# One subtraction per step on GpSimd, low products a step later, first key tiles loaded earlier, in a two-layer graph attention kernel

## The chip, the cores and the metric

The kernel runs on one core of a Trainium2 chip. The metric is the device time of one execution in microseconds (us), as the median of several runs. An engine is named by its role: TensorE (PE in the profile), VectorE (DVE), ScalarE (ACT), GpSimd (POOL), SyncE (SP, which issues DMA transfers).

## The reference

```python
# x: 4096 x 512, adj: 4096 x 4096; both layers: h = relu(layernorm(x)), 8 heads of 64
# layer 0: leaky additive scores + adj, softmax, times the projected rows; added to x
...
# layer 1, added to x again
keys = jnp.einsum('nj,hjk->hnk', node_matrix, Wks)
queries = jnp.einsum('nj,hjk->hnk', node_matrix, Wqs)
values = jnp.einsum('nj,hjk->hnk', node_matrix, Wvs)
atts = jnp.einsum('hqk,hmk->hqm', queries, keys) / key_dim ** 0.5
atts = atts - 1e+16 * (1.0 - adj)[None, :, :]
atts = jax.nn.softmax(atts, axis=-1)
return jnp.einsum('hqm,hmk,hko->qo', atts, values, Wo)
```

The diff concerns layer 1 alone.

## The kernel before, in words

`build` runs four stages one after another: projection and attention of layer 0, then `layer1_project` and `layer1_attention`. Each stage is a block in which every engine has its own hand-written instruction order; engines meet only through semaphores that count, and a stage ends when all its engines are done.

**Numbers.** Scores and sums need more precision than one fp16 product gives, so operands are split in a high and a low fp16 part. Keys are kept twice: KA holds, for each parity of head pair and each head x, the high part on partitions 0 to 63 and the low part on 64 to 127; KB holds the high part on partitions 0 to 63, and constant rows that carry the negated row maximum. The exponential of a score tile is written twice by ScalarE: in fp32 to PF (L1550) and in fp16 to PH (L1554). PL = PF - PH is the low part, subtracted by GpSimd, one tile of 128 x 512 an instruction (`split`, L1501 to L1505).

**`layer1_project`** walks 8 blocks of 512 rows. SyncE stores each query and key tile (high and low) to DRAM scratch (L989), loads the finished 512 columns of the first head pair's keys to KA's parity 0 (`load_first_keys`, L969 to L977), stores the V tiles (L995) and in block 0 loads queries. TensorE and VectorE use those first keys for the first head pair's guards (below, L1197 and L1072) within this stage.

**`layer1_attention`** walks NB = 8 blocks of 512 query rows, in each HP = 4 head pairs, in each NT = 32 key tiles of 128 rows: a *step* is one key tile for both heads of a pair, 1024 steps in all, two tiles (t) a step. The order of a step on TensorE (`body`, L1807 to L1843):

- `scores` for x = 0 and 1: two 512-column matmuls each (L1740, L1741) into one of three PSUM banks, and a third (L1743) that adds the mask, unless VectorE adds it (L1683; in pair 0 every second tile, later 3 of 8). A bank is free when the exponential of three tiles before is done.
- *guards*: score matmuls of the **next** head pair without softmax (L1724), 64 a head pair in steps 1 to 28, of which VectorE takes masked row maxima (L1594). After the last one VectorE reduces them (L1602) and negates and scales them (L1604, `merge_guards`); in step 30 TensorE turns them into a row (`crow`, L1729 to L1733), which VectorE writes into QL (L1610) for the next pair's scores.
- `products` of the step LAG = 2 before: 16 high matmuls of 65 or 64 columns with PH (L1761, L1763), then 8 low ones of 65 columns with PL (L1771), which wait for GpSimd. At their end the step counts as used, which frees slots of PH and PL (8 tiles) and pieces of V.
- `finish` for the pair before: its accumulators are copied in step 2 (ScalarE L1530, VectorE L1615), normalised in step 3 (L1621 reciprocal, L1623 multiply), transposed in step 5 (L1780), split in step 7 (L1629, L1631), and after the fourth pair multiplied by Wo (L1789, 48 matmuls).

ScalarE takes tiles in order: wait for the scores or VectorE's mask, wait for PF's slot (4 tiles, freed by GpSimd), L1550, L1554. VectorE's order is written by hand too: finish, guard maxima, masks. In the last two head pairs of a block it also sets up masks of the next one (`mask_setup` L1572, L1575; `mask_diagonal` L1583). SyncE's queue reloads KA, KB, V, masks and queries group by group (a group is 8 key tiles) as they come free; at the start of the stage it issues, for each of 4 groups, KB of the first pair, the mask MT, V, and KA of the second pair (L1428 to L1434). Guards from step 1 on read KA of the second pair.

Of the kernel before, what the change touches and what calls it, by code (L numbers as in the profile page):

```python
# [885 lines left out]
def layer1_project(nc, T, DR):  # L886
# [4 lines left out]
    with ExitStack() as ctx:  # L891
# [10 lines left out]
        s_KA, s_Q, s_MR, s_dblk, s_mk, s_fill = (T[name] for name in ("s_KA", "s_Q", "s_MR", "s_dblk", "s_mk", "s_fill"))  # L902
# [48 lines left out]
        def _(sp):  # L951
# [26 lines left out]

            load_first_rows()
# [3 lines left out]
            for g in range(NB):  # L983
                for j in range(PAIRS):

                    sp.wait_ge(s_lo, g * PAIRS + (j + 1))
                    row, i, to = (j % HP) * P, j % RING, "qk"[j // HP]
                    for half, tile in (("h", hi), ("l", lo)):
                        sp.dma_start(DR[to + half][row:row + P, bass.ds(g * QB, QB)], tile[:, i, :]).then_inc(s_qout[i], 16)  # L989
                if g == 0:  # L990
                    load_first_queries(0)
                load_first_keys(g)
                for s in range(SUB):
                    sp.wait_ge(s_v, g * SUB + (s + 3))
                    sp.dma_start(DR["v1"][:, bass.ds(g * QB + s * P, P), :].rearrange("h p k -> p h k"),  # L995
                                 vt[:, s, :, :].rearrange("p (h a) k -> p h (a k)", a=2)).then_inc(s_vout, 16)
                if g == 0:
                    load_first_queries(1)
            for i in range(RING):
                sp.wait_ge(s_qout[i], 32 * (NB * PAIRS // RING + 1))  # L1000
# [254 lines left out]
def layer1_attention(nc, T, DR):  # L1255
# [11 lines left out]
    F_RING, H_RING = 4, 8  # L1267
# [36 lines left out]
    POOL_SLOTS = (0, 1, 2, 3)  # L1304
    PER_RING = (F_RING - len(POOL_SLOTS), len(POOL_SLOTS))
    SPLITS = tuple(n * TILES // F_RING for n in PER_RING)

# [7 lines left out]
    def keys_landed(par, count):  # L1315

        return 64 * (count + (2 if par == 0 else 1))

    def by_pool(t):
        return t % F_RING in POOL_SLOTS  # L1320

    def split_count(t):

        return sum(by_pool(k) == by_pool(t) for k in range(t + 1))

    with ExitStack() as ctx:
# [10 lines left out]
        s_KA, s_Q, s_MR, s_dblk, s_mk, s_fill = (T[name] for name in ("s_KA", "s_Q", "s_MR", "s_dblk", "s_mk", "s_fill"))  # L1337
# [25 lines left out]
        s_KB = [sem(f"kb_in{i}") for i in range(GROUPS)]  # L1363
# [5 lines left out]
        s_low = sem("low_by_vector")  # L1369
# [57 lines left out]
        def _(sp):  # L1427
            sp.dma_start(idh[:, :], DR["idh"]).then_inc(s_fill, 16)  # L1428
            for i in range(GROUPS):
                load_kb(sp, 0, i)  # L1430
                load_mt(sp, 0, i)
                load_v(sp, 0, i)
                load_ka(sp, 1, 1, i)
# [55 lines left out]
            for par in range(2):  # L1489
                for i in range(GROUPS):  # L1490
                    sp.wait_ge(s_KA[par][i], keys_landed(par, 2 * NB))
            for hp in range(HP):
                sp.wait_ge(s_Q[hp], 96 * (NB + (1 if hp < 2 else 0)))
            for i in range(GROUPS):
                sp.wait_ge(s_KB[i], 32 * (HP * NB + 1))
                sp.wait_ge(s_V[i], 16 * (HP * NB + (1 if i < GROUPS - 1 else 0)))
                sp.wait_ge(s_MT[i], 16 * (NB + (1 if i < GROUPS - 1 else 0)))
# [3 lines left out]
        def split(eng, engine, nb, t):  # L1501

            engine.wait_ge(s_P, nb * TILES + (CREDIT + t + 1))
            eng.tensor_tensor(PL[:, t % H_RING, :], PF[:, t % F_RING, :], PH[:, t % H_RING, :],  # L1504
                              ALU.subtract).then_inc(s_lowp if by_pool(t) else s_low, 1)  # L1505

        @block.gpsimd
        def _(pool):
            pool.memset(shift[D:D + 2, :], P_SHIFT / C_ROW).then_inc(s_fill, 1)
            pool.sem_inc(s_lowp, PER_RING[1])  # L1510
            for nb in range(NB):
                for t in range(TILES):
                    if by_pool(t):
                        split(nc.gpsimd, pool, nb, t)

        @block.scalar
        def _(act):
# [14 lines left out]
            def body(nb, first):  # L1532
                for hp in range(HP):
                    for mb in range(NT):
# [7 lines left out]
                        for x in range(2):  # L1542
                            t = hp * PAIR + 2 * mb + x
                            if masked_by_vector(t):
                                act.wait_ge(s_M, nb * vector_masks(TILES - 1) + vector_masks(t))
                            else:
                                act.wait_ge(s_S, nb * TILES + (CREDIT + t + 1))

                            act.wait_ge(s_lowp if by_pool(t) else s_low, nb * SPLITS[by_pool(t)] + split_count(t))
                            nc.scalar.activation(PF[:, t % F_RING, :], sc[(nb * TILES + t) % BANKS][:, :], ACT.Exp, scale=EXP_SCALE)  # L1550

                            if x == 0:
                                act.wait_ge(s_used, nb * STEPS + (hp * NT + mb + 1))
                            nc.scalar.activation(PH[:, t % H_RING, :], sc[(nb * TILES + t) % BANKS][:, :], ACT.Exp, scale=EXP_SCALE).then_inc(s_P, 1)  # L1554
# [6 lines left out]
        def _(dve):  # L1561
            nc.vector.tensor_copy(only[D:D + 2, :], T["identf"][D:D + 2, D:D + 2]).then_inc(s_set, 1)
            nc.vector.tensor_scalar(idm[:, :], T["identf"][:, :], -MASK_FLOOR, None, ALU.mult).then_inc(s_set, 1)
            if PER_RING[0]:
                dve.sem_inc(s_low, PER_RING[0])
# [97 lines left out]
            def body(nb, first):  # L1663
                for hp in range(HP):
                    for mb in range(NT):
# [6 lines left out]
                        for x in range(2):  # L1672
                            t = 2 * (step - 1) + x
                            if t >= 0 and not by_pool(t):
                                split(nc.vector, dve, nb, t)
                            elif t < 0 and not first and not by_pool(t + TILES):
                                split(nc.vector, dve, nb - 1, t + TILES)
# [24 lines left out]
            for x in range(2):  # L1702
                if not by_pool(TILES - 2 + x):
                    split(nc.vector, dve, NB - 1, TILES - 2 + x)
# [4 lines left out]
        def _(pe):  # L1709
# [4 lines left out]
            def guard(it, nxt, gi, count, blk):  # L1714
# [4 lines left out]
                if s == 0 and x == 0 and c % (MC // GROUPS) == 0:  # L1719
                    pe.wait_ge(s_KA[par][c // (MC // GROUPS)], keys_landed(par, count))  # L1720
# [25 lines left out]
            def products(nb, step):  # L1746
# [9 lines left out]
                first, last = mb == 0, mb == NT - 1  # L1756
# [16 lines left out]
                mm.then_inc(s_used, 1)  # L1773

# [32 lines left out]
            def body(nb, first):  # L1807
                for hp in range(HP):
                    for mb in range(NT):
                        step = hp * NT + mb  # L1810
                        if mb == 0:
                            count = nb * 2 + hp // 2
                            pe.wait_ge(s_Q[hp], nb * 96 + 96)
                            for i in range(GROUPS):
                                pe.wait_ge(s_KA[hp % 2][i], keys_landed(hp % 2, count))

                            pe.wait_ge(s_crowc, nb * (2 * HP) + (2 * hp + 2))
                        if mb % PER == 0:
                            pe.wait_ge(s_KB[mb // PER], nb * (32 * HP) + 32 * (hp + 1))
# [33 lines left out]
def build(nc, DR):  # L1853

    with ExitStack() as ctx:
# [25 lines left out]
        T["s_KA"] = [[ctx.enter_context(nc.semaphore(f"d_ka_in{par}{i}")) for i in range(4)] for par in range(2)]  # L1881
        T["s_Q"] = [ctx.enter_context(nc.semaphore(f"d_q_in{i}")) for i in range(HP)]
# [39 lines left out]
```

## Time and profile before

| | us |
|---|---|
| median of 3 runs | 4457.64 (4455.89 to 4460.37) |
| the profiled execution | 4473.09, its span 4471.2 |
| attention of layer 1 within that span | from 1930.7 to the end |
| TensorE busy, share of the span | 4331.6, 97% |
| VectorE, ScalarE, GpSimd busy | 3661.4, 3249.5, 3425.5 |
| L1504 subtraction, 2048 times | 2316.8 |

A busy time is the union of an engine's instructions as the profiler saw them; a matmul's end is modelled and overlaps the next one's start, so TensorE's pace is read from starts. In a row of a timeline stand the start from the span's beginning, the length, engine, line, operation, the tile written and those read, and the count of instructions merged in it; in brackets the idle time before it and what ended it. "SPq" is SyncE's issuing of a transfer. PEld is the weight load of a matmul. In a row of a window stand its length, then the busy time and instruction count of PE, PEld, DVE, ACT and POOL, then the granted TensorE clock as a share of full speed, the DMA engines' mean busy share, and GB/s.

### The profile page before, as it was taken

To read this page: it belongs to the slowest core of one execution; us is meant where nothing else is said; L and a number is where in the kernel's file an instruction comes from. 1 tells how busy PE (TensorE), PEld (TensorE's weight loads), DVE (VectorE), ACT (ScalarE), POOL (GpSimd) and SP (SyncE) were. 2 spreads that over 40 slices of the span, in tenths; PEclk is the share of its full clock that TensorE was granted. 3 is DMA by queue.
4 is the path that set the end of the run, shared out by engine and by line. 5 is a ranking of instruction groups with operands and counts; after the bars stand their busy time and mean duration, and the time that the engine had idled before them with its cause. 6 is when DMAs were issued, how large, how long until landed. Compare 5 with 4: busy or idle time off the path is not lost.

```text
span 4471.2 us, 111742 instructions
## 1 busy us (share of the span) xinstructions
PE 4331.6 (97%) x42956; PEld 2088.0 (47%) x42956; DVE 3661.4 (82%) x7790; ACT 3249.5 (73%) x6022; POOL 3425.5 (77%) x2955
## 2 busy tenths in 40 slices
PE   8899999999999979979999999999999999999998
PEld 4322222222222224435656656656666566566565
DVE  5799999998999855558888878888888888788886
ACT  5566666666666643348878878888888788888786
POOL 2567677676776740049989989989999899899897
PEclk9999999999999989989999999999999999999999
DMA  5467777677676544353433433333334334334333
GB/s 164 166 192 225 213 228 208 197 225 216 208 213 198 164 158 141 119 149 88 132 87 110 133 97 108 113 107 116 107 95 129 94 97 136 92 111 130 101 107 107
DMA packets 464214, 646.06 MB, mean 144 GB/s; under 512 B 49792, under 2 KB 273408, under 8 KB 453568
## 3 DMA queue, kind: packets, MB, share of 16 engines
q1 hardware_dynamic: 385248, 522.36, 38.4%
q10 hardware_dynamic: 73856, 100.83, 8.3%
q0 software_dynamic: 4576, 15.73, 1.1%
q8 instruction: 338, 5.54, 0.5%
q14 instruction: 196, 1.61, 0.1%
HBM read 528.38 MB, written 110.38 MB: 143 GB/s over the span
## 4 chain that ended last, share of the span: by engine, by line
PE 43%; POOL 7%; DVE 2%; ACT 2%; issue 2%; SPq 1%; DMA 0%; DVEq 0%; POOLq 0%; ACTq 0%
PE d_gd L1724 9%; PE d_sc L1740 8%; PE d_sc L1741 7%; POOL d_PL L1504 7%; PE d_sc L1743 4%; PE d_acc L1761 4%; PE d_acc L1763 4%; PE d_acc L1771 4%; PE d_misc L1789 2%; ACT d_PH L1554 1%; DVE d_junk L1594 1%; DVE d_sc L1683 1%; ACT d_PF L1550 0%; PE d_misc L1780 0%; SPq L1392 0%
## 5 line engine op out<-in xcount | busy, mean ns | idle before, releaser
L1504 POOL TENSOR_TENSOR d_PL<-d_PF,d_PH 128x512 f16<-128x512 f32 x2048 | 2316.8, 1166 | 198.1 <-ACT d_PH L1554 194.8
L1594 DVE CUSTOM_DVE_ANT_0 d_junk<-d_gd,d_MR 128x512 bf16<-128x512 f32 x2048 | 1396.5, 688 | 410.9 <-PE d_gd L1724 406.1
L1550 ACT ACTIVATE d_PF<-d_sc 128x512 f32<-128x512 f32 x2048 | 1261.0, 616 | 401.1 <-DVE d_sc L1683 304.7
L821 DVE SCALAR_TENSOR_TENSOR b_P<-R,u,b_A 128x512 f32<-128x512 f32 x1792 | 1197.5, 739 | 98.6 <-ACT b_A L674 50.6
L1554 ACT ACTIVATE d_PH<-d_sc 128x512 f16<-128x512 f32 x2048 | 1270.6, 620 | 0.0
L867 PE MATMUL b_acc<-b_P,V 128*64 128x512 f32 x4096 | 949.7, 605 | 30.5 <-ACT b_oT L742 19.2
L1724 PE MATMUL d_gd<-d_KA,d_QA 128*128 128x512 f16 x2048 | 779.0, 380 | 23.2 <-DMA d_KA<-scratch_kl 17.0
L1740 PE MATMUL d_sc<-d_QA,d_KA 128*128 128x512 f16 x2048 | 778.3, 380 | 11.1 <-DMA d_MT<-scratch_mt 4.9
L1741 PE MATMUL d_sc<-d_QL,d_KB 128*128 128x512 f16 x2048 | 777.7, 380 | 0.0
L1761 PE MATMUL d_acc<-d_V,d_PH 128*128 128x65 f16 x8192 | 640.1, 193 | 1.7 <-ACT d_PH L1554 0.2
L1763 PE MATMUL d_acc<-d_V,d_PH 128*128 128x64 f16 x8192 | 641.0, 194 | 0.0
L1761 PEld LDWEIGHTS d_acc<-d_V,d_PH 128*128 128x128 f16 x8192 | 577.9, 98 | 118.1 <-ACT d_oC L1530 15.0
L1683 DVE SCALAR_TENSOR_TENSOR d_sc<-d_MT,d_sc 128x512 f32<-128x512 bf16 x832 | 574.8, 691 | 29.4 <-PE d_sc L1741 28.4
L1763 PEld LDWEIGHTS d_acc<-d_V,d_PH 128*128 128x128 f16 x8192 | 541.1, 97 | 113.8 <-issue 0.8
L867 PEld LDWEIGHTS b_acc<-b_P,V 128*64 128x64 f32 x4096 | 276.7, 138 | 674.4 <-issue 393.2
L639 POOL TENSOR_TENSOR b_P<-b_G,b_AS 128x512 f32<-128x512 f32 x256 | 328.0, 1281 | 323.9 <-PE b_den L874 173.0
L874 PE MATMUL b_den<-b_P,V 128*2 128x512 f32 x4096 | 485.9, 592 | 0.0
L1743 PE MATMUL d_sc<-d_MT,d_idm 128*128 128x512 bf16 x1216 | 461.6, 380 | 0.0
L674 ACT ACTIVATE b_A<-stage 128x512 f32<-128x512 f32 x256 | 152.9, 597 | 415.0 <-DVE b_P L821 342.9
L1771 PE MATMUL d_acc<-d_V,d_PL 128*128 128x65 f16 x8192 | 414.5, 193 | 2.2 <-POOL d_PL L1504 2.2
L621 POOL TENSOR_TENSOR b_D<-stage,b_rm 128x512 f32<-128x512 f32 x256 | 330.8, 1292 | 50.4 <-DMA stage<-in_adjT 44.3
L1724 PEld LDWEIGHTS d_gd<-d_KA,d_QA 128*128 128x128 f16 x2048 | 199.9, 98 | 288.7 <-DVE d_gm L1594 82.7
(140 smaller groups left out, 4188.2 us busy)
## 6 DMA issues: line engine op xcount, KB each, us to landing
d_V<-scratch_v SPq DMA_DIRECT2D x131, 520.0 KB, 4.3
stage<-in_adjT SPq DMA_DIRECT2D x128, 512.0 KB, 5.9
b_srow<-in_adj ACTq DMA_DIRECT2D x256, 256.0 KB, 4.1
b_rows<-in_adj SPq DMA_DIRECT2D x112, 512.0 KB, 5.2
d_MR<-scratch_mr SPq DMA_DIRECT2D x36, 1024.0 KB, 5.9
d_MT<-scratch_mt SPq DMA_DIRECT2D x35, 1024.0 KB, 6.8
d_KB<-scratch_kh SPq DMA_DIRECT2D x264, 128.0 KB, 3.3
d_KA<-scratch_kh SPq DMA_DIRECT2D x264, 128.0 KB, 3.0
```

What stands on the lines that cost most here:

```text
L821: nc.vector.scalar_tensor_tensor(out=PT[:, m % P_STEPS, h, :], in0=R[:, par, h, :], scalar=T["u"][:, m, h:h + 1], in1=A[m % A_RING][:, :], ...
L867: nc.tensor.matmul(acc[h // 2][x * D:(x + 1) * D, :], T["V"][:, m, h, 0:D], PT[:, m % P_STEPS, h, :], start=(m == 0), stop=(m == NT - 1))
L1504: eng.tensor_tensor(PL[:, t % H_RING, :], PF[:, t % F_RING, :], PH[:, t % H_RING, :], ALU.subtract).then_inc(s_lowp if by_pool(t) else s_l ...
L1550: nc.scalar.activation(PF[:, t % F_RING, :], sc[(nb * TILES + t) % BANKS][:, :], ACT.Exp, scale=EXP_SCALE)
L1554: nc.scalar.activation(PH[:, t % H_RING, :], sc[(nb * TILES + t) % BANKS][:, :], ACT.Exp, scale=EXP_SCALE).then_inc(s_P, 1)
L1594: nc.vector.tensor_tensor_reduce(out=junk[:, gi % 2, :], in0=gd[gi % 2][:, :], in1=MR[:, s, c * QB:(c + 1) * QB], scale=1.0, scalar=-3.0e3 ...
L1724: nc.tensor.matmul(gd[gi % 2][:, :], QA[:, nxt, x, s * P:(s + 1) * P], KA[:, par, x, c * QB:(c + 1) * QB], start=True, stop=True).then_inc ...
L1740: nc.tensor.matmul(bank, KA[:, par, x, mb * P:(mb + 1) * P], QA[:, hp, x, :], start=True, stop=False)
L1741: mm = nc.tensor.matmul(bank, KB[:, x, mb * P:(mb + 1) * P], QL[:, hp, x, :], start=False, stop=not own)
L1743: mm = nc.tensor.matmul(bank, idm[:, :], MT[:, mb, :], start=False, stop=True)
L1761: nc.tensor.matmul(acc[x][:, s * K:(s + 1) * K], rows, V[:, mb, x, 0:K], start=first and s == 0, stop=False, skip_group_check=True)
L1763: nc.tensor.matmul(acc[x][:, s * K:s * K + D], rows, V[:, mb, x, VL:VK], start=False, stop=False, skip_group_check=True)
```

## The change

Three things are done. (1) `layer1_project` gets a second loader that fills, behind each block's V stores, KB for the first head pair and KA for the second; the stage after it issues neither, and the semaphores of KB move with it. (2) GpSimd subtracts both tiles of a step in one instruction of 128 x 2 x 512, once both exponentials are done; PF has 6 slots. (3) `products` is split: the low products of a step go ahead of the high products of the next one, three steps behind the scores, save for a head pair's last step, whose low products stay behind its high ones. The code for subtractions by VectorE, of which none was used, goes.

```diff
@@ layer1_project, SyncE
+            def load_next_keys(c):
+
+                sp.wait_ge(s_qout[1], 32 * (2 * c + 3))
+                if c % 2:
+                    sp.wait_ge(s_KA[1][c // 2], 64)
+                    sp.wait_ge(s_KB[c // 2], 32)
+                cols = slice(c * QB, (c + 1) * QB)
+                for x in range(2):
+                    sp.dma_start(KB[0:D, x, cols], DR["kh"][x * D:(x + 1) * D, cols]).then_inc(s_KB[c // 2], 16)
+                for x in range(2):
+                    row = (2 + x) * D
+                    sp.dma_start(KA[0:D, 1, x, cols], DR["kh"][row:row + D, cols]).then_inc(s_KA[1][c // 2], 16)
+                    sp.dma_start(KA[D:P, 1, x, cols], DR["kl"][row:row + D, cols]).then_inc(s_KA[1][c // 2], 16)
...
                 if g == 0:
                     load_first_queries(1)
+                load_next_keys(g)
@@ layer1_attention
-    F_RING, H_RING = 4, 8
+    F_RING, H_RING = 6, 8
...
             for i in range(GROUPS):
-                load_kb(sp, 0, i)
                 load_mt(sp, 0, i)
                 load_v(sp, 0, i)
-                load_ka(sp, 1, 1, i)
...
@@ GpSimd
-            pool.sem_inc(s_lowp, PER_RING[1])
             for nb in range(NB):
-                for t in range(TILES):
-                    if by_pool(t):
-                        split(nc.gpsimd, pool, nb, t)
+                for step in range(STEPS):
+                    pool.wait_ge(s_P, nb * TILES + (CREDIT + 2 * step + 2))
+                    full = (nb * TILES + 2 * step) % F_RING
+                    half = 2 * step % H_RING
+                    nc.gpsimd.tensor_tensor(PL[:, half:half + 2, :], PF[:, full:full + 2, :], PH[:, half:half + 2, :], ALU.subtract).then_inc(s_lowp, 1)
@@ ScalarE
-                            act.wait_ge(s_lowp if by_pool(t) else s_low, nb * SPLITS[by_pool(t)] + split_count(t))
-                            nc.scalar.activation(PF[:, t % F_RING, :], sc[(nb * TILES + t) % BANKS][:, :], ACT.Exp, scale=EXP_SCALE)
+                            if nb * TILES + t >= F_RING:
+                                act.wait_ge(s_lowp, nb * STEPS + (t - F_RING) // 2 + 1)
+                            nc.scalar.activation(PF[:, (nb * TILES + t) % F_RING, :], sc[(nb * TILES + t) % BANKS][:, :], ACT.Exp, scale=EXP_SCALE)
@@ TensorE
-            def products(nb, step):
+            def products_high(nb, step):
...
+            def products_low(nb, step):
+                mb = step % NT
+                last = mb == NT - 1
+                pe.wait_ge(s_lowp, nb * STEPS + step + 1)
                 for x in range(2):
                     t = 2 * step + x
-                    own = by_pool(t)
-                    pe.wait_ge(s_lowp if own else s_low, nb * SPLITS[own] + (PER_RING[own] + split_count(t)))
                     for s in range(SUB):
                         mm = nc.tensor.matmul(acc[x][:, s * K:(s + 1) * K], PL[:, t % H_RING, s * P:(s + 1) * P], V[:, mb, x, 0:K],
                                               start=False, stop=last, skip_group_check=True)
                 mm.then_inc(s_used, 1)
+
+            def products(nb, step):
+
+                mb = step % NT
+                if mb:
+                    products_low(nb, step - 1)
+                products_high(nb, step)
+                if mb == NT - 1:
+                    products_low(nb, step)
```

The counts in `keys_landed`, in the wait for KB (now `hp + 2`) and in the waits at the stage's end follow the moved loads.

## Rows read from the trace of the kernel before

**Rows 1.** Busy time by engine in the window of one head pair
```profile
3050.28:3125.54 75.26, 74.91 (x1009) 46.24 (x1008) 64.80 (x166) 65.57 (x130) 72.28 (x66) 1.00 0.46 137
```

**Rows 2.** Timeline of TensorE (start us, us, engine, line, operation, tiles, count)
```profile
1905.45 2.75 PE L1229 MATMUL c_qp<-c_hT,c_wkS 128*128 128x512 f16 x12
...
3044.03 0.20 PE L1761 MATMUL d_acc<-d_V,d_PH 128*128 128x65 f16 x1
...
3044.53 0.40 PE L1771 MATMUL d_acc<-d_V,d_PL 128*128 128x65 f16 x8
...
3044.77 0.38 PE L1740 MATMUL d_sc<-d_QA,d_KA 128*128 128x512 f16 x1
...
3045.21 0.38 PE L1743 MATMUL d_sc<-d_MT,d_idm 128*128 128x512 bf16 x1
...
3045.67 0.39 PE L1740 MATMUL d_sc<-d_QA,d_KA 128*128 128x512 f16 x1
```

**Rows 3.** Timeline of GpSimd, five and two subtractions back to back
```profile
2998.40 5.62 POOL L1504 TENSOR_TENSOR d_PL<-d_PF,d_PH 128x512 f16<-128x512 f32 x5
...
3040.61 2.27 POOL L1504 TENSOR_TENSOR d_PL<-d_PF,d_PH 128x512 f16<-128x512 f32 x2
```

**Rows 4.** Line L1771: what TensorE idled for before its low products
```profile
  POOL d_PL L1504: 4.7, 6
```

**Rows 5.** Waits between 1931 and 2010 us (total us, times, longest)
```profile
PE d_gd L1724 <- DMA d_KA<-scratch_kl: 17.0, 4, 7.8
```

**Rows 6.** Busy time between 1940 and 1970 us (columns as in rows 1)
```profile
1940.00:1970.00 30.00, 12.99 (x75) 5.61 (x74) 6.60 (x16) 8.96 (x18) 10.28 (x9) 0.67 1.05 275
```

**Rows 7.** DMA issues between 1930 and 1962 us (KB each, us to landing)
```profile
d_KA<-scratch_kl SPq DMA_DIRECT2D x8, 128.0 KB, 7.2
...
d_MT<-scratch_mt SPq DMA_DIRECT2D x4, 1024.0 KB, 9.8
```

**Rows 8.** Timeline where the projection ends and the attention starts
```profile
1895.40 0.33 SPq L989 DMA_DIRECT2D scratch_qh<-c_hi  x1
...
1918.56 7.35 SPq L995 DMA_DIRECT2D scratch_v<-c_vt  x4
...
1930.69 0.35 SPq L1428 DMA_DIRECT2D d_idh<-in_idh  x1
...
1932.22 0.59 SPq L1423 DMA_DIRECT2D d_MT<-scratch_mt  x1
...
1937.93 0.59 PE L1740 MATMUL d_sc<-d_QA,d_KA 128*128 128x512 f16 x1 [4.87 <-DMA d_MT<-scratch_mt]
...
1975.15 0.38 PE L1740 MATMUL d_sc<-d_QA,d_KA 128*128 128x512 f16 x1
```

**Rows 9.** Timeline of GpSimd: its smallest memset
```profile
1930.69 0.09 POOL L1509 MEMSET d_shift<- 2x1 f32 x1 [83.06 <-POOLq L891]
```

**Rows 10.** Lines L1604 and L1623: duration ns least, median, most, first and last start
```profile
L1604 DVE TENSOR_SCALAR d_cmh<-d_cm x33: 174/883/965, 1931.4 to 4437.4; 128x8 f16<-128x8 f32 x33
...
L1623 DVE TENSOR_TENSOR d_oR<-d_oC,d_rd x32: 692/856/1599, 2045.4 to 4446.8; 128x512 f32<-128x512 f32 x32
```

**Rows 11.** Timeline from step 29 of a head pair to step 4 after
```profile
3042.03 0.89 DVE L1604 TENSOR_SCALAR d_cmh<-d_cm 128x8 f16<-128x8 f32 x1
...
3043.54 0.60 ACT L1550 ACTIVATE d_PF<-d_sc 128x512 f32<-128x512 f32 x1 [0.88 <-DVE d_sc L1683]
...
3047.85 0.70 ACT L1554 ACTIVATE d_PH<-d_sc 128x512 f16<-128x512 f32 x1
...
3051.02 0.41 PE L1771 MATMUL d_acc<-d_V,d_PL 128*128 128x65 f16 x8
...
3054.49 0.85 DVE L1623 TENSOR_TENSOR d_oR<-d_oC,d_rd 128x512 f32<-128x512 f32 x1
...
3056.47 0.68 DVE L1594 CUSTOM_DVE_ANT_0 d_junk<-d_gd,d_MR 128x512 bf16<-128x512 f32 x1
...
3057.34 0.38 PE L1724 MATMUL d_gd<-d_KA,d_QA 128*128 128x512 f16 x1
```

More of the change, by code:

```diff
@@ L901, in layer1_project @@
         KA, QA, QL, KB, MR, dblk, brow, gm, junk = (T[name] for name in ("KA", "QA", "QL", "KB", "MR", "dblk", "brow", "gm", "junk"))
-        s_KA, s_Q, s_MR, s_dblk, s_mk, s_fill = (T[name] for name in ("s_KA", "s_Q", "s_MR", "s_dblk", "s_mk", "s_fill"))
+        s_KA, s_KB, s_Q, s_MR, s_dblk, s_mk, s_fill = (T[name] for name in ("s_KA", "s_KB", "s_Q", "s_MR", "s_dblk", "s_mk", "s_fill"))
         MC = N // QB
@@ L1302, in layer1_attention @@
     ROW_SET = [(HP - 1) * NT + late for late in (-2, -1, 0, 3)]
-    POOL_SLOTS = (0, 1, 2, 3)
-    PER_RING = (F_RING - len(POOL_SLOTS), len(POOL_SLOTS))
-    SPLITS = tuple(n * TILES // F_RING for n in PER_RING)
     def masked_by_vector(t):
@@ L1313, in vector_masks, with keys_landed @@
         return sum(masked_by_vector(k) for k in range(t + 1))
[L1315 to L1324, printed above, removed]
+    def keys_landed(count):
+        return 64 * (count + 2)
     with ExitStack() as ctx:
@@ L1336, in layer1_attention @@
         KA, QA, QL, KB, MR, dblk, brow, gm, junk = (T[name] for name in ("KA", "QA", "QL", "KB", "MR", "dblk", "brow", "gm", "junk"))
-        s_KA, s_Q, s_MR, s_dblk, s_mk, s_fill = (T[name] for name in ("s_KA", "s_Q", "s_MR", "s_dblk", "s_mk", "s_fill"))
+        s_KA, s_KB, s_Q, s_MR, s_dblk, s_mk, s_fill = (T[name] for name in ("s_KA", "s_KB", "s_Q", "s_MR", "s_dblk", "s_mk", "s_fill"))
         V = sb("d_V", [P, NT, 2, VK], F16)
@@ L1362, in layer1_attention @@
         s_oNh = sem("normalised_high")
-        s_KB = [sem(f"kb_in{i}") for i in range(GROUPS)]
         s_V = [sem(f"v_in{i}") for i in range(GROUPS)]
@@ L1368, in layer1_attention @@
         s_P = sem("exp_done")
-        s_low = sem("low_by_vector")
         s_lowp = sem("low_by_gpsimd")
@@ L1490, in _ @@
                 for i in range(GROUPS):
-                    sp.wait_ge(s_KA[par][i], keys_landed(par, 2 * NB))
+                    sp.wait_ge(s_KA[par][i], keys_landed(2 * NB))
             for hp in range(HP):
@@ L1494, in _ @@
             for i in range(GROUPS):
-                sp.wait_ge(s_KB[i], 32 * (HP * NB + 1))
+                sp.wait_ge(s_KB[i], 32 * (HP * NB + 2))
                 sp.wait_ge(s_V[i], 16 * (HP * NB + (1 if i < GROUPS - 1 else 0)))
@@ L1499, in _ @@
                 sp.wait_ge(s_MR[s], 16 * (NB + 1))
[L1501 to L1505, printed above, removed]
         @block.gpsimd
@@ L1563, in _ @@
             nc.vector.tensor_scalar(idm[:, :], T["identf"][:, :], -MASK_FLOOR, None, ALU.mult).then_inc(s_set, 1)
-            if PER_RING[0]:
-                dve.sem_inc(s_low, PER_RING[0])
             dve.sem_inc(s_acv, 1)
@@ L1672, in body @@
                         for x in range(2):
[L1673 to L1677, printed above, removed]
                             t = 2 * step + x
@@ L1701, in _ @@
                 body(nb, nb == 0)
-            for x in range(2):
-                if not by_pool(TILES - 2 + x):
-                    split(nc.vector, dve, NB - 1, TILES - 2 + x)
             for mb in range(NT):
@@ L1719, in guard @@
                 if s == 0 and x == 0 and c % (MC // GROUPS) == 0:
-                    pe.wait_ge(s_KA[par][c // (MC // GROUPS)], keys_landed(par, count))
+                    pe.wait_ge(s_KA[par][c // (MC // GROUPS)], keys_landed(count))
                 if gi >= 2 or not isinstance(it, int):
@@ L1755, in products @@
                 pe.wait_ge(s_P, nb * TILES + (CREDIT + 2 * step + 2))
-                first, last = mb == 0, mb == NT - 1
+                first = mb == 0
                 for x in range(2):
@@ L1814, in body @@
                             for i in range(GROUPS):
-                                pe.wait_ge(s_KA[hp % 2][i], keys_landed(hp % 2, count))
+                                pe.wait_ge(s_KA[hp % 2][i], keys_landed(count))
                             pe.wait_ge(s_crowc, nb * (2 * HP) + (2 * hp + 2))
                         if mb % PER == 0:
-                            pe.wait_ge(s_KB[mb // PER], nb * (32 * HP) + 32 * (hp + 1))
+                            pe.wait_ge(s_KB[mb // PER], nb * (32 * HP) + 32 * (hp + 2))
                             if hp == 0:
@@ L1881, in build @@
         T["s_KA"] = [[ctx.enter_context(nc.semaphore(f"d_ka_in{par}{i}")) for i in range(4)] for par in range(2)]
+        T["s_KB"] = [ctx.enter_context(nc.semaphore(f"d_kb_in{i}")) for i in range(4)]
         T["s_Q"] = [ctx.enter_context(nc.semaphore(f"d_q_in{i}")) for i in range(HP)]
```

## The prediction, made before the changed kernel was run

> **What bounds the kernel now.** I first took the busy times of one head pair of layer 1's attention [rows 1]: of 75.26 us TensorE is busy 74.91, GpSimd 72.28, VectorE 64.80, ScalarE 65.57. Ends of matmuls are modelled, so I went on by starts [rows 2]. Twelve 512-column matmuls span 2.75 us, so they follow each other after (2.75 - 0.38)/11 = 0.216 us; the 16 high matmuls of a step take 0.50 us (3044.03 to 3044.53), the 8 low ones 0.24 (to 3044.77). A head pair has 32 steps: 128 score, 40 mask and 64 guard matmuls make 232 x 0.216 = 50.1 us, high products 16.0, low ones 7.7, transposes and the row of maxima some 0.7: 74.5 us. So TensorE has under 1 us of stall in a head pair of 75.26, and a stall added to it is paid in full. GpSimd is second: back to back, five subtractions span 5.62 us and two 2.27, a pitch of 1.117 us and 1.15 for one [rows 3], 71.5 us per head pair; in the whole run it kept TensorE waiting six times, 4.7 us in all [rows 4]. More speed on GpSimd buys nothing.
>
> The one large hole is the start of this attention: TensorE waits 17.0 us for the second parity's keys [rows 5] and 4.87 us for the first mask group [rows 8]; over 30 us there the DMA engines are full (share 1.05, 275 GB/s) and the granted clock is 0.67 [rows 6], in between its levels of 1.2 and 2.4 GHz, as it falls after each idle wait.
>
> **Part 1, keys loaded in the projection.** The first loads of the attention were 24 key transfers (16 KA, 8 KB) of 128 KB among 4 mask groups of 1 MB [rows 7], 2 MB of V and 1 MB of Wo: 10.2 MB, at 275 GB/s 37 us. Without the keys the first mask group is issued 1.1 us earlier, at 1931.1, and needs at most the 5.7 us of before (1932.22 to the score at 1937.93 [rows 8]), so scores start near 1936.4. The work of steps 0 to 5, from the prices above, is 1.1 + 1.5 + 2.0 + 2.2 + 2.5 + 2.2 = 11.5 us. I let the clock rise 4.5 us after the first score, as it did before (matmuls spaced 0.43 us until 1942.4): 2.2 us of work by 1940.9, and the other 9.3 us end at 1950.2. Before, the score of step 6 began at 1975.15 [rows 8]. **Gain 25 us**, between 21 (the clock low for twice as long) and 27. The later groups of mask and V take 5.5 us each and are wanted 19 us apart: no wait moves there. What pays: SyncE issues six transfers more per block of the projection, 0.64 us each, 3.8 us, behind the V stores and ahead of the next block's first query store. Even all 3.8 us late (1895.4 before [rows 8]), that store is out long before its buffer is wanted again, four tiles of about 3 us on: nothing. In the last block the V stores end at 1925.9, so the six are out at 1929.8, before the attention's first issue at 1930.69 [rows 8]: nothing, at most 1 us for a late landing. Taking the keys out of SyncE's queue in the attention delays nobody. Together 0, bounds 0 and 2 us.
>
> **Part 2, one subtraction of 2 x 512.** The trace has none of 1024 elements. Upper bound of the pitch: twice 1.117 = 2.23 us. Lower: the smallest memset takes 0.09 us [rows 9]; if that much is fixed, 2.15. I take 2.23, the subtraction's own row. The Trainium skill (GPSIMD Engine Reference, Elementwise — side-by-side cycle accounting) has 4497 ns for 2048 elements; an estimate from it and the 1.15 us for 512 would be 2.27 us long, 0.04 saved. As GpSimd isn't the limit, this saves nothing by itself. What changes is how long one instruction holds what VectorE also wants. The negation of the maxima (L1604, 8 elements a partition) takes 174 ns with GpSimd idle and 883 at the median; the normalising multiply (L1623) 692 at the least and 856 [rows 10]. In the timeline L1604 starts at 3042.03 and ends at 3042.92 [rows 11]; the second subtraction of step 28 starts 1.12 after 3040.61 and ends at 3042.88 [rows 3]. So it waits for that instruction's end, and it meets it 0.30 us after its start in every head pair.
>
> A pair of step 28 would start at the same place (its second tile and the pair before are both done by 3041.7), but end 1.11 us later, so L1604 lasts 2.0 us. Behind it on VectorE stands the mask of step 29, for which ScalarE already waits 0.88 us [rows 11]; from 3043.54 on ScalarE works back to back, 1.92 us a step, into the next head pair, and TensorE waits for its banks (3045.21 to 3045.67 where 0.216 would do [rows 2]). That chain is critical already, so the 1.11 us reach TensorE. **Cost 32 x 1.11 = 35 us**, bounds 0 (below) and 37.
>
> L1623, at step 3, starts at 3054.49 and loses some 0.3 us to a subtraction. With pairs GpSimd is behind at that place, as steps 29 to 0 bring a pair every 1.92 us against 2.23, and L1623 meets one about 1.0 us after its start: 1.2 us lost. Behind it are the maxima, back to back: the one begun at 3056.47 ends at 3057.15, and the guard that needs it stands at 3057.34 [rows 11], 0.2 us of slack. **Cost 32 x 0.6 = 19 us**, bounds 0 and 32. The four diagonal masks of a row block (L1583) are of the same kind: 8 x 0.5 = 4 us, bounds 0 and 10.
>
> **Part 3, low products one step later.** The matmuls stay the same, and within a head pair the wait for GpSimd is covered by a step more. The last step's low products keep their distance of two: before they began at 3051.02, 2.47 us after their exponential's end at 3048.55 [rows 11]. Now that is 2.7, but GpSimd is 0.6 behind and takes 2.27, so its result is there after 2.9. **Cost 32 x 0.25 = 8 us**, bounds 0 and 15. In exchange step 1 carries eight low matmuls more and step 2 none, so the high products of step 2 find the accumulator copied: 0.1 us each, -4 us. At the end the last subtraction ends 1.1 us later: +1. PF has 6 slots for 4, which ScalarE hardly waited for: nothing. The V loads wait for "used" one step later and are needed over 20 steps on: nothing.
>
> **Sum**: -25 + 35 + 19 + 4 + 8 - 4 + 1 = +38 us on the profiled execution's 4473.1, which stands 15.5 above the median of 4457.6; on the median it gives **4496 us**.
>
> **Rivals.** (a) *The hold doesn't grow*: VectorE is let in between the two halves, or L1604 falls into a gap. No row refuses the first, since all subtractions in them are 512 long. Then -25 + 8 - 4 + 1 = -20: 4438 us. Against the gap: a pair would have to be over 2.3 us long to fall so far behind that it begins after L1604. The Trainium skill (SBUF — State Buffer, Who interferes with whom) has the shared ports held for the whole instruction and the second to issue blocked fully; by that the hold doubles, which is my sum. (b) *Half as bad*: L1623's loss falls into slack and L1604's is partly made up: 4460 to 4475. (c) *Worse*: every hold costs its bound, -25 + 37 + 32 + 10 + 15 - 4 + 1 = +66: 4524 us. (d) *The start is bound by masks and clock*, not by keys: it gains 15: 4506 us. Between faster and slower it is the hold that decides: with less than (25 - 5)/32 = 0.6 us of new stall in a head pair, L1604's and L1623's together, the start wins.
>
> **How the numbers follow.** Forecast with (d) 0.58, (c) 0.07, (b) 0.08, (a) 0.27. Under 0.2%, 9 us, no difference can be told. Faster comes from (a), less the case that it loses 11 us elsewhere: 0.23. Same, from the rest of (a) and the low end of (b): 0.08. Slower 0.69. The forecast's own range is 4465 to 4522; to hold 8 in 10 it must reach into (a): 4438 to 4522.
>
> **What would show it.** L1604 near 2.0 us and L1623 near 1.7 at the median, both ending with a subtraction; TensorE's gaps before the scores of steps 31 and 0 longer by 1.1 us, those of step 4 by 0.6; a head pair of 77.2 us for 75.3; no wait for keys, and the first L1604 of the loop some 25 us nearer the start; subtractions x1024 at a pitch of 2.2 to 2.25. If L1604 stays at 0.9, (a) holds and part 2 is wrong; if it is 2.0 and a head pair stays at 75.3, the chain from it to TensorE has slack that I missed.

## The result and the profile after

The changed kernel takes 4476.2 us at the median (4473.7 to 4478.1, 6 runs), the kernel before, in the same comparison, 4459.6 us (4455.9 to 4463.3, 6 runs). The ratio is 1.0036, with a 95% interval of 1.0024 to 1.0048: slower by 16.6 us, where I had forecast 38.

The spans of the two profiled executions hardly differ (4471.2 and 4471.9 us), since the one of before spent some 15 us more before the last projection, in code that the change leaves alone. So I compare from the first negation of maxima on, which stands at the attention's start and then once in each of the 32 head pairs. Its line in the changed kernel, with those of the other VectorE instructions at issue and of the subtraction (duration ns least, median, most; first and last start):

```profile
L1599 DVE TENSOR_SCALAR d_cmh<-d_cm x33: 174/1717/1853, 1918.7 to 4436.4; 128x8 f16<-128x8 f32 x33
...
L1618 DVE TENSOR_TENSOR d_oR<-d_oC,d_rd x32: 692/1007/1191, 2009.0 to 4447.5; 128x512 f32<-128x512 f32 x32
...
L1578 DVE TENSOR_SCALAR d_MR<-d_dblk,d_brow x32: 329/993/2170, 2153.5 to 4376.4; 128x128 bf16<-128x128 f32 x32
...
L1510 POOL TENSOR_TENSOR d_PL<-d_PF,d_PH x1024: 2121/2133/4182, 1927.8 to 4444.1; 128x1024 f16<-128x1024 f32 x171
```

Against [rows 10]: the negation (L1604 before, L1599 now) went from 883 to 1717 ns, the normalising multiply (L1623, now L1618) from 856 to 1007. From first to last negation before took 4437.4 - 1931.4 = 2506.0 us, after 4436.4 - 1918.7 = 2517.7: 11.7 more. What follows the last one takes 4471.2 - 4437.4 = 33.8 us before and 35.5 after, so the profiles hold 13.4 us of the 16.6.

The 32 intervals between negations show where it lies. The first was 98.6 us and is now 73.1: the start's gain, 25.5 us. The others fall into four kinds by the head pair's place in its block of queries, as the first of a block has more to do. Their means over the last twenty-eight, seven of each kind:

| interval between starts of the negation, us | first of a block | second | third | fourth |
|---|---|---|---|---|
| before | 85.06 | 75.23 | 75.22 | 75.58 |
| after | 86.29 | 76.47 | 76.34 | 76.79 |

Every kind is 1.1 to 1.2 us longer, some 37 us over the 31 intervals behind the first.

The attention's start, in the timeline of the changed kernel (columns as in [rows 2]):

```profile
1918.34 0.42 SPq L1425 DMA_DIRECT2D d_MT<-scratch_mt  x1
...
1923.61 0.59 PE L1727 MATMUL d_sc<-d_QA,d_KA 128*128 128x512 f16 x1 [3.02 <-DMA d_MT<-scratch_mt]
...
1926.12 0.56 PE L1728 MATMUL d_sc<-d_QL,d_KB 128*128 128x512 f16 x1
1926.52 0.38 PE L1730 MATMUL d_sc<-d_MT,d_idm 128*128 128x512 bf16 x1
```

The first mask group is awaited for 3.02 us, scores start 5.27 us after its issue (5.71 before, [rows 8]), the granted clock goes from the lower to the upper level 2.9 us after the first score (matmuls 0.43 us apart until 1926.1, 0.22 from 1926.5), and no wait for keys is left where there were 17.0 us [rows 5]. The window of thirty microseconds behind it, and that of one head pair (columns as in [rows 1]):

```profile
1928.00:1958.00 30.00, 29.68 (x394) 18.05 (x399) 27.13 (x73) 27.38 (x55) 28.58 (x14) 1.00 0.65 205
2387.40:2463.70 76.30, 74.32 (x994) 46.14 (x1008) 63.03 (x162) 65.84 (x129) 68.14 (x33) 1.00 0.41 121
```

In the first, TensorE is busy 29.68 of 30 us at a granted clock of 1.00, against 12.99 and 0.67 in [rows 6]. In the second, its 74.32 us of work stand in 76.30 us: some 2 us without work, where [rows 1] showed 0.35. Part of that is no stall, since the trace lacks 511 records of the mask's matmul L1730, so I count stalls by starts.

Where that stall sits, around a negation in the middle of the run:

```profile
2385.40 4.22 POOL L1510 TENSOR_TENSOR d_PL<-d_PF,d_PH 128x1024 f16<-128x1024 f32 x2
...
2387.94 1.72 DVE L1599 TENSOR_SCALAR d_cmh<-d_cm 128x8 f16<-128x8 f32 x1
2389.57 1.28 DVE L1673 SCALAR_TENSOR_TENSOR d_sc<-d_MT,d_sc 128x512 f32<-128x512 bf16 x2
...
2390.28 0.60 ACT L1547 ACTIVATE d_PF<-d_sc 128x512 f32<-128x512 f32 x1 [1.71 <-DVE d_sc L1673]
...
2391.42 0.39 PE L1727 MATMUL d_sc<-d_QA,d_KA 128*128 128x512 f16 x1 [0.49 <-ACT d_PH L1551]
...
2392.40 0.39 PE L1727 MATMUL d_sc<-d_QA,d_KA 128*128 128x512 f16 x1 [0.16 <-ACT d_PH L1551]
```

Read it from above. Two subtractions take 4.22 us, one alone 2.13, so the second starts at 2385.40 + 2.09 = 2387.49 and ends at 2389.62. The negation starts 0.45 us after it and ends at 2389.66, 0.04 after it. Only then comes the mask, whose result ScalarE has awaited for 1.71 us (0.88 in [rows 11]), and behind ScalarE TensorE waits for a bank of scores. I took the start of every matmul of layer 1's attention and added up what exceeds its kind's usual spacing: before, TensorE lost 1.37 us in a head pair, after 2.52. Of the 1.15 us more, 0.79 stand at step 30, the next one behind the negation, and 0.34 at step 4, where the guards wait for VectorE behind the multiply.

### The profile page after: what moved, and what is told of

It reads as the page before. It is cut to its first block, busy times and chain, and to the rows that moved or that the text cites. A ratio compares the mean times of both kernels' runs of the same rounds, so it can differ in the third digit from the quotient of the medians.

```text
span 4471.9 us, 110228 instructions
## 1 busy us (share of the span) xinstructions
PE 4295.6 (96%) x42445; PEld 2081.9 (47%) x42956; DVE 3700.8 (83%) x7790; ACT 3249.1 (73%) x6022; POOL 3292.7 (74%) x1931
## 4 chain that ended last, share of the span: by engine, by line
PE 46%; DVE 6%; issue 3%; ACT 2%; DMA 0%; POOL 0%; POOLq 0%; DVEq 0%; ACTq 0%; SPq 0%
PE d_gd L1711 11%; PE d_sc L1727 8%; PE d_sc L1728 8%; PE d_acc L1750 5%; PE d_acc L1748 5%; PE d_acc L1760 5%; PE d_sc L1730 3%; PE d_misc L1787 2%; DVE d_junk L1589 2%; DVE d_sc L1673 2%; DVE d_cmh L1599 1%; ACT d_PH L1551 1%; ACT d_PF L1547 1%; DVE d_MR L1578 1%; PE d_misc L1778 0%
## 5 line engine op out<-in xcount | busy, mean ns | idle before, releaser
L1510 POOL TENSOR_TENSOR d_PL<-d_PF,d_PH 128x1024 f16<-128x1024 f32 x1024 | 2183.7, 2147 | 344.6 <-ACT d_PH L1551 307.9
L1748 PEld LDWEIGHTS d_acc<-d_V,d_PH 128*128 128x128 f16 x8192 | 539.4, 98 | 10.3 <-ACT d_oC L1526 10.1
L1750 PEld LDWEIGHTS d_acc<-d_V,d_PH 128*128 128x128 f16 x8192 | 539.1, 97 | 1.3
L1760 PEld LDWEIGHTS d_acc<-d_V,d_PL 128*128 128x128 f16 x8192 | 380.3, 97 | 215.7 <-POOL d_PL L1510 2.8
```

The lines of the kernel that those rows point to most:

```text
L1510: nc.gpsimd.tensor_tensor(PL[:, half:half + 2, :], PF[:, full:full + 2, :], PH[:, half:half + 2, :], ALU.subtract).then_inc(s_lowp, 1)
L1748: nc.tensor.matmul(acc[x][:, s * K:(s + 1) * K], rows, V[:, mb, x, 0:K], start=first and s == 0, stop=False, skip_group_check=True)
L1750: nc.tensor.matmul(acc[x][:, s * K:s * K + D], rows, V[:, mb, x, VL:VK], start=False, stop=False, skip_group_check=True)
L1760: mm = nc.tensor.matmul(acc[x][:, s * K:(s + 1) * K], PL[:, t % H_RING, s * P:(s + 1) * P], V[:, mb, x, 0:K], start=False, stop=last, skip ...
```

## The experiments

Each ratio is to the kernel before as it ran beside that run, with medians of 4464.4 to 4467.4 us, and not to the 4459.6 above.

**1 and 2: each part alone.** The first kernel is the one before with the key loads moved and nothing else; the second is the changed one with the key loads put back (`load_kb` and `load_ka` in the attention's first block, `load_next_keys(g)` out).

> The kernel before with the key loads moved into the projection, and nothing else. Theory H (the pair subtraction holds what VectorE wants for longer, and that alone costs): start of the attention 25 us shorter, projection 2 us longer, head pairs 75.2 to 75.6 us as before, so 4436 us for 4459, ratio 0.995; L1604's line stays at 0.88 us. Rival R (the keys' early transfers themselves disturb the head pairs or the start gains less): over 4445 us.

> The changed kernel with the key loads back in the attention: pair subtraction and later low products alone. Theory H: head pairs 76.3 to 76.8 us for 75.2 to 75.6, 31 of them, 2 us at the end: +39 us, 4498 us, ratio 1.009. Rival R: under 4480 us.

Keys only: 4442.7 us (5 runs), ratio 0.9943 (0.9931 to 0.9956), 25 us faster. Pairs only: 4508.5 us (5 runs), ratio 1.0089 (1.0075 to 1.0103), 40 us slower. Their sum, +14, is the change's +16.6 within the intervals. The negation's line, keys only and then pairs only:

```profile
L1616 DVE TENSOR_SCALAR d_cmh<-d_cm x33: 174/882/959, 1925.2 to 4405.9; 128x8 f16<-128x8 f32 x33
```

```profile
L1600 DVE TENSOR_SCALAR d_cmh<-d_cm x33: 174/1717/1853, 1928.4 to 4474.5; 128x8 f16<-128x8 f32 x33
```

Keys only has its intervals as before to 0.01 us (85.06, 75.23, 75.21, 75.58) and its first at 73.4; pairs only has the changed kernel's (86.29, 76.47, 76.33, 76.79) and its first at 101.6, 3.0 more than before. So the parts add up, and the loss is the pairs' alone.

**3: one instruction in 32 split again.** If the hold at the negation is the loss, it is enough to halve the one subtraction that the negation meets:

```
 for step in range(STEPS):
...
-    nc.gpsimd.tensor_tensor(PL[:, half:half + 2, :], ..., ALU.subtract).then_inc(s_lowp, 1)
+    if step % NT == 28:
+        for x in range(2):
+            nc.gpsimd.tensor_tensor(PL[:, half + x, :], ..., ALU.subtract).then_inc(s_lowp, 1)
+    else:
+        nc.gpsimd.tensor_tensor(PL[:, half:half + 2, :], ..., ALU.subtract).then_inc(s_lowp, 1)
```

> The changed kernel, but step 28 of each head pair is subtracted in two instructions of 512 instead of one of 1024: one instruction in 32 differs. Theory H: the negation of the maxima waits for the end of a 1.15 us instruction instead of a 2.13 us one, 0.7 to 0.9 us instead of 1.72, and TensorE's stall at step 30 goes back by 0.8 us a head pair: 25 us less than the changed kernel, 4451 us. Rival L (the new order of the low products makes the stalls of steps 30 and 31): within 4 us of the changed kernel, 4473 to 4480.

4462.1 us (11 runs), ratio 0.9989 (0.9980 to 0.9998): 21 us less than the changed kernel, by the two ratios. Timeline at one negation, then two lines of it:

```profile
2387.24 2.28 POOL L1516 TENSOR_TENSOR d_PL<-d_PF,d_PH 128x512 f16<-128x512 f32 x2
...
2387.69 0.74 DVE L1607 TENSOR_SCALAR d_cmh<-d_cm 128x8 f16<-128x8 f32 x1
```

```profile
L1607 DVE TENSOR_SCALAR d_cmh<-d_cm x33: 174/745/883, 1921.6 to 4422.1; 128x8 f16<-128x8 f32 x33
...
L1586 DVE TENSOR_SCALAR d_MR<-d_dblk,d_brow x32: 278/304/2191, 2154.0 to 4362.0; 128x128 bf16<-128x128 f32 x32
```

The first of the halves ends 1.14 us before the second's end, at about 2388.38, and the negation at 2388.43. Step 30 loses 0.21 us again instead of 1.01, and the first three kinds of interval give back 0.97 each (85.32, 75.50, 75.37). The fourth doesn't (77.41): there the masks of the diagonal now meet a pair (up to 2191 ns), and step 0 loses 0.55 us. A split at one place moves what GpSimd does at the next.

**4: the converse.** Keys only, with one pair in 32, at step 28:

```
 for t in range(TILES):
+    if t % PAIR == 56:
+        pool.wait_ge(s_P, nb * TILES + (CREDIT + t + 2))
+        h, f = t % H_RING, t % F_RING
+        nc.gpsimd.tensor_tensor(PL[:, h:h + 2, :], PF[:, f:f + 2, :], PH[:, h:h + 2, :], ALU.subtract).then_inc(s_lowp, 2)
-    if by_pool(t):
+    elif t % PAIR != 57:
         split(nc.gpsimd, pool, nb, t)
```

> The keys-only kernel (singles of 512 throughout), but the two tiles of step 28 of each head pair are subtracted in one instruction: the counterpart of the run before. Theory H: that one long hold makes L1604's line last 1.7 us instead of 0.88 and costs TensorE 0.8 us at step 30 in each head pair, 25 us on the keys-only kernel: its ratio to the kernel before rises from 0.994 to 1.000. Rival: pairs cost through their number (GpSimd's latency in every step), so one in 32 costs under 5 us, ratio under 0.996.

4469.8 us (11 runs), ratio 1.0010 (1.0001 to 1.0018): 30 us slower than keys only by the ratios, 27 by the intervals (85.82, 76.25, 75.98, 76.35).

```profile
L1620 DVE TENSOR_SCALAR d_cmh<-d_cm x33: 174/1650/1923, 1930.7 to 4437.3; 128x8 f16<-128x8 f32 x33
```

Thirty-two joined instructions, in place of 64 of the 2048, cost what all of the start's gain is worth, and step 30 loses 0.97 us. Together with run 3 that settles the cause of the larger share.

**5: the order of the low products.** The changed kernel with low products two steps behind, as before (`products_high(nb, step)`, then `products_low(nb, step)`, for every step).

> The changed kernel, but with the low products two steps behind the scores in every step, as before the change; subtractions in pairs. Theory H: the pair of subtractions ends about 2.2 us after the exponentials and before, low products began 2.5 to 3.5 us after them, so most steps have no wait; steps 29 to 2 of a head pair, 2.0 to 2.5 us in the kernel before, wait a few tenths: +0 to +15 us on the changed kernel. Rival L: the order was what cost, so 20 us or more less than the changed kernel.

4481.7 us (6 runs), ratio 1.0031 (1.0019 to 1.0042): no difference from the changed kernel. The intervals are alike too (86.28, 76.53, 76.41, 76.97), though the stalls lie elsewhere: step 31 loses 0.5 us more, step 4 loses 0.3 less. So the step of distance that the change adds does two things that cancel. What it does at step 4 shows in the first score of step 3 and the multiply behind it, in the changed kernel and then in this run:

```profile
2400.24 0.38 PE L1727 MATMUL d_sc<-d_QA,d_KA 128*128 128x512 f16 x1
...
2401.47 1.00 DVE L1618 TENSOR_TENSOR d_oR<-d_oC,d_rd 128x512 f32<-128x512 f32 x1
```

```profile
2410.80 0.38 PE L1727 MATMUL d_sc<-d_QA,d_KA 128*128 128x512 f16 x1
...
2411.69 0.91 DVE L1618 TENSOR_TENSOR d_oR<-d_oC,d_rd 128x512 f32<-128x512 f32 x1
```

With the new order the multiply starts 1.23 us after that score in three head pairs of four, with the old one 0.90 in three of four, and in the kernel before 0.7 to 0.9. So most of the loss at step 4 needs the new order beside the longer subtraction. The new order with subtractions of 512 was not run.

**6 and 7: the negation on ScalarE.** If the hold is the cause, the negation has to leave VectorE. It goes in front of ScalarE's second tile of step 29:

```
+def negate_max(it):
+    act.wait_ge(s_cm, 2 * it + 1)
+    nc.scalar.activation(cmh[:, :, :].rearrange("p s x -> p x s"), cm[:, :, :], ACT.Copy, scale=-1.0 / C_ROW).then_inc(s_cm, 1)
...
-    nc.vector.tensor_scalar(cmh[:, :, :].rearrange("p s x -> p x s"), cm[:, :, :], -1.0 / C_ROW, None, ALU.mult).then_inc(s_cm, 1)
```

Once in the changed kernel, once in keys only:

> The changed kernel with the negation of the maxima on ScalarE, between the two tiles of step 29, instead of on VectorE; everything else, pairs too, stays. Theory H: ScalarE doesn't share GpSimd's ports, the negation takes about 0.2 us and the mask of step 29 is no longer late. TensorE's stalls at steps 30 and 31 (1.3 us a head pair) fall to 0.3 or less; the ones at step 4 stay: 30 us less than the changed kernel, ratio to the kernel before 0.997. Rival (the pair itself slows the chain by its latency): within 8 us of the changed kernel.

> The keys-only kernel with the negation on ScalarE: subtractions of 512. Theory H: the stalls of steps 30 and 31, 0.56 us a head pair in the kernel before, are due to the same hold and mostly go: 10 to 17 us less than keys only, ratio to the kernel before 0.991. Rival (those stalls are ScalarE's own pace): no change from keys only, 0.994.

In the changed kernel it gives 4439.7 us (5 runs), ratio 0.9945 (0.9934 to 0.9957), a larger gain than I had expected:

```profile
L1521 ACT ACTIVATE d_cmh<-d_cm x33: 208/210/231, 1924.7 to 4406.3; 128x8 f16<-128x8 f32 x33
```

The negation takes 210 ns whatever GpSimd does, step 30 loses 0.18 us, and the intervals (84.61, 74.63, 74.78, 77.06; from here on between starts of the reduction ahead of the negation, where ScalarE negates) are as short on average, 77.77, as those of keys only, whose negation still waits 0.88 us. So this edit alone takes back all that the pairs had cost.

In keys only it is a miss: 4463.2 us (12 runs), ratio 0.9993 (0.9983 to 1.0003), 22 us slower than keys only by the ratios, 14 by the intervals; its single times spread over 19 us. Three kinds of interval are shorter (84.48, 74.59, 75.33 for first, second and fourth), the third is 78.48. The normalising multiply's line, and the timeline at one multiply of the second interval and at one of the third:

```profile
L1640 DVE TENSOR_TENSOR d_oR<-d_oC,d_rd x32: 692/774/3849, 2019.3 to 4435.9; 128x512 f32<-128x512 f32 x32
```

```profile
2332.20 2.73 POOL L1516 TENSOR_TENSOR d_PL<-d_PF,d_PH 128x512 f16<-128x512 f32 x2
2333.17 0.74 DVE L1640 TENSOR_TENSOR d_oR<-d_oC,d_rd 128x512 f32<-128x512 f32 x1
...
2406.77 4.51 POOL L1516 TENSOR_TENSOR d_PL<-d_PF,d_PH 128x512 f16<-128x512 f32 x4
2407.99 3.85 DVE L1640 TENSOR_TENSOR d_oR<-d_oC,d_rd 128x512 f32<-128x512 f32 x1
```

The multiply of 0.74 us started 0.97 us after a subtraction and was let in at its end; the next subtraction was longer for it (the two took 2.73 us, not 2.27). The one of 3.85 us started 0.1 us after a subtraction's start (2406.77 + 1.12 = 2407.89) and stood while that one and two more ran on at their usual pace, the four in 4.51 us. It ended only after GpSimd had stopped, for want of work: its next subtraction came 2.96 us later.

**8: the cost of a shorter instruction.** Keys only, each subtraction in two of 256 (`for c in (slice(0, QB // 2), slice(QB // 2, QB))`, counts doubled). It tells the fixed cost per instruction apart from the cost per element.

> The keys-only kernel with each tile subtracted in two instructions of 256: a measurement of what an instruction costs apart from its elements. The pitches seen, 1.117 us for 512 and 2.087 for 1024, put 0.147 us aside and 1.895 ns an element: 0.63 us for 256, 2.53 a step. GpSimd then bounds the head pairs: 32 x 2.53 = 81 us each, some 150 us more in all. If the cost were only 0.04 us an instruction, 256 would take 0.58 and a head pair stay near 75 to 76 us.

A single execution, 4761.7 us. Timeline of GpSimd, then lines of VectorE:

```profile
2999.82 1.93 POOL L1517 TENSOR_TENSOR d_PL<-d_PF,d_PH 128x256 f16<-128x256 f32 x3
...
3001.90 2.56 POOL L1517 TENSOR_TENSOR d_PL<-d_PF,d_PH 128x256 f16<-128x256 f32 x4 [0.15 <-ACT d_PH L1566]
```

```profile
L1635 DVE TENSOR_TENSOR d_oR<-d_oC,d_rd x32: 691/5299/5885, 2026.5 to 4735.6; 128x512 f32<-128x512 f32 x32
...
L1616 DVE TENSOR_SCALAR d_cmh<-d_cm x33: 174/1522/4609, 1929.8 to 4723.6; 128x8 f16<-128x8 f32 x33
```

Four take 0.63 us more than three: that is the pitch for 256, and with 1.117 for 512 [rows 3] and 2.09 for 1024 it lies on a line of 0.147 us an instruction and 1.895 ns an element. GpSimd, at 2 x 0.63 x 64 = 81 us a head pair, is now the bound, and I expected intervals of 81. They are 93.8, 87.1, 85.4 and 84.8, as the multiply stands for 5.3 us behind subtractions that come back to back.

**9 and 10: both small instructions off VectorE.** The negation on ScalarE, and the multiply in GpSimd's own queue behind the subtractions of step 2:

```
+def normalise_by_pool(n):
+    pool.wait_ge(s_oN, 2 * n + 2)
+    nc.gpsimd.tensor_tensor(oR[:, :, :].rearrange("p s (x d) -> p x s d", x=2), oC[:, :, :, 0:D],
+                            rd[:, :, :, :].to_broadcast([P, 2, SUB, D]), ALU.mult).then_inc(s_oN, 1)
```

Once with keys only, once with the whole change:

> Keys only, subtractions of 512, negation on ScalarE, and the normalising multiply on GpSimd behind the subtractions of step 2, so that VectorE has no two-input or fast-mode instruction left in most of a head pair. In the run without the last edit that multiply lasted 3.85 us in one head pair of four, beginning 0.1 us after a subtraction, and 0.7 in the others. Theory H (it is kept out by GpSimd's back-to-back instructions): head pairs of 74.6 to 75.3 us with no exception, 15 to 22 us less than keys only, ratio to the kernel before 0.990 to 0.991. Rival (moving the negation costs ScalarE time that comes back elsewhere): 0.994 or more.

> The changed kernel with both edits: negation on ScalarE, multiply on GpSimd behind the pair of step 2. Theory H: the stall at step 4 (0.22 us a head pair) goes; what is left against the kernel before is the diagonal masks, that wait up to 2 us for a pair at the last head pair of a block: 5 to 10 us less than the changed kernel with the negation alone on ScalarE, ratio to the kernel before 0.992 to 0.9935, some 10 us more than the same with subtractions of 512. Rival (pairs are better once nothing waits for them, as GpSimd has 0.15 us more in each step): below the run with 512.

Keys only: 4430.0 us (5 runs), ratio 0.9924 (0.9910 to 0.9938), faster than both kernels of the comparison. With pairs: 4439.5 us (5 runs), ratio 0.9941 (0.9929 to 0.9953). Lines of the first, then one of the second:

```profile
L1546 ACT ACTIVATE d_cmh<-d_cm x33: 208/210/232, 1930.4 to 4400.5; 128x8 f16<-128x8 f32 x33
...
L1526 POOL TENSOR_TENSOR d_oR<-d_oC,d_rd x32: 1032/1046/1065, 2022.7 to 4408.7; 128x512 f32<-128x512 f32 x32
```

```profile
L1593 DVE TENSOR_SCALAR d_MR<-d_dblk,d_brow x32: 280/540/1960, 2159.8 to 4343.5; 128x128 bf16<-128x128 f32 x32
```

The multiply takes 1.05 us on GpSimd, every time, and the third interval is back at 74.81. Both gains are smaller than I had expected: against keys only 8 us by the ratios, not 15 to 22, as the first interval is 1 us longer and the fourth no shorter (75.78 for 75.58); and with pairs the second edit is worth 2 us on run 6, which the intervals of the ratios don't tell from nothing. The two kernels have the same intervals within 0.1 us but for the fourth, 75.78 against 76.74: with pairs the diagonal's masks wait up to 1.96 us at step 0. That is what pairs still cost, 8 us by the intervals and 8 by the ratios, whose own intervals just overlap.

## Why the prediction was right in sign and off in size

**The bound held.** I said that a stall added to TensorE is paid in full. The starts give 1.15 us more stall in a head pair and the intervals 1.1 to 1.2.

**Part 1 held, 25 forecast, 25.5 in the first interval and 25 by run 1.** The mask group came 0.4 us sooner than the 5.7 us I allowed, and the clock rose 2.9 us after the first score, not 4.5. The six transfers more per block cost nothing that I found: SyncE had sent the last of them off by 1917.2 and the first of the attention went at 1917.94. The matmuls of the last projection take 284.4 us in the changed kernel and 282.4 before, but pairs only, without those transfers, has the 284.4 as well, and run 5, with them, has 282.3.

**Part 2 is where the size went wrong.** The mechanism is as put: the negation ends with the subtraction that it meets, ScalarE and TensorE wait in turn, in every head pair, and runs 3 and 4 show it from both sides. The step that failed is "I take 2.23, the subtraction's own row". Measured, a subtraction of 1024 is 2.13 us long with a pitch of 2.09, below even my lower bound of 2.15: the smallest memset [rows 9] was no bound for the fixed part, 0.147 us. The estimate of 2.27 that I drew from the Trainium skill (GPSIMD Engine Reference, Elementwise — side-by-side cycle accounting) was further off still. With it fell "A pair of step 28 would start at the same place": the negation meets the pair 0.45 us after its start, not 0.30. So it is held 1.717 - 0.883 = 0.83 us more, not 1.11; 0.14 of the difference is the pair's length (2.13, where two subtractions take 2.27 [rows 3]) and 0.14 the earlier start. Step 30 loses 0.79: 25 us, for my 35.

The multiply's term was wrong in more than that. Already "loses some 0.3 us" was misread: the row's 0.85 is 0.16 above the least, 0.69. GpSimd, with 2.09 us against ScalarE's 1.92 instead of 2.23, falls less behind, and the multiply meets its subtraction 1.5 to 1.7 us after its start, not 1.0; it lasts 1007 ns at the median, 0.15 us more than before, where I had 1.7 us. Step 4 still loses 0.34 us: 11 us, for my 19. That is more than the 0.15, and run 5 shows why it isn't the hold's alone: with the same pairs and multiplies of 0.9 to 1.0 us, but the old order, that loss is nearly gone. So only a part of the 11 us is the mechanism that I had priced. The masks of the diagonal did double (466 ns at the median before, 993 after), but step 0 lost only 0.02 us a head pair more: 1 us, for my 4.

**Part 3 came to nothing.** My +8 rested on "0.6 behind" and 2.27 us of length, both from the same term; between head pairs no wait of the last low products for GpSimd shows, and at the stage's end they wait 2.4 us, 1.4 before, which is part of the tail. The -4 for the high products of step 2 didn't come on the average either: that step loses 0.18 us against 0.16, less in three head pairs of four and some 0.5 more in the fourth of a block. Run 5 says the same of the whole part as a sum, with a cost at step 4 that I had not seen and a gain at step 31. The tail is 1.7 us longer, for 1.

So the sum by its own terms is -25.5 + 25 + 11 + 1 + 1.7 = +13, and 13.4 is what the profiles hold. The median's 16.6, 10.7 to 21.4 by its interval, has room for it.

**The rivals.** (a), that the hold doesn't grow, is refuted: the negation took 1717 or 1718 ns at the median in every run with pairs throughout and the negation on VectorE. Here the trace agrees with the Trainium skill (SBUF — State Buffer, Who interferes with whom), that the second of the two is blocked until the first's instruction is over; runs 7 and 8 show where that isn't the whole story. (b) came nearest in time, 4460 to 4475, for a reason that is half right: the multiply's loss was smaller, but not since it fell into slack. (c) and (d) are refuted by the step stalls and by run 1. My threshold, 0.6 us of new stall in a head pair to undo the start's gain, I would put at 25.5/32 = 0.8; it was 1.15.

**What stays open.** How the 0.34 us at step 4 divide between the longer subtraction and the order. Why a waiting two-input instruction of VectorE is let in behind one subtraction in one case and stands through three or eight in another. And why pairs only has 3 us in its first interval more than before, of which 1.2 are the hold.

## What to carry to other kernels

Before two instructions on GpSimd are joined into one, look for the small VectorE instructions that start while one is in course and for what is queued behind them: here one subtraction in 32, grown from 1.1 to 2.1 us, cost 27 us of 4460. Move such an instruction to an engine that isn't held (the negation: 883 or 1717 ns on VectorE, 210 on ScalarE), and look afterwards at the next VectorE instruction that GpSimd may now meet at another phase, since taking out one stall shifts everything behind it. Measure the fixed cost of an instruction by two sizes of the same instruction before a bound rests on another kind's.

## What the runs showed of the hardware that I had not expected

GpSimd's subtraction of two f32 or f16 operands into f16 fits 0.147 us + 1.895 ns an element at 256, 512 and 1024 elements (pitches of 0.627, 1.117 and 2.087 us).

A multiply of 692 ns on VectorE stood for 3.85 us behind subtractions of 1.15 us, and for 5.3 us at the median behind those of 0.68: several instructions of GpSimd in a row, each of which it might have been let in between. In run 8 the longest negation took 4.6 us for 174 ns of work. Shorter instructions on GpSimd are thus no sure cure for the hold. In the pair of cases laid side by side, the instruction let in behind one subtraction had started 0.97 us into a subtraction and the other 0.1 us, but that isn't what decides. The first multiply of the same run starts 0.11 us into a subtraction (2016.92 + 2 x 1.117 = 2019.15) and is let in at that one's end:

```profile
2016.92 4.96 POOL L1516 TENSOR_TENSOR d_PL<-d_PF,d_PH 128x512 f16<-128x512 f32 x4
...
2019.26 1.60 DVE L1640 TENSOR_TENSOR d_oR<-d_oC,d_rd 128x512 f32<-128x512 f32 x1
```

So is the first of the kernel before, also 0.11 us into one and 1.60 us long. A multiply let in so ends 0.55 us after the end of the subtraction that it met (up to 0.62 where it met only the last of it), behind short and long ones alike.
